# Two cross-attention layers: scores computed a second time in transposed form, heads in groups of four

## The chip, the cores and the metric

The kernel runs on one core of a Trainium2 chip. The core has TensorE (matrix products, into the PSUM banks), VectorE, ScalarE, GpSimd, and SyncE, whose queue issues most of the DMAs. The metric is the device time of one execution in microseconds, the median of the runs.

## The reference

Sixteen sequences ("batches") of 112 tokens of width 320 pass two cross-attention layers over a context of 375 tokens of width 192. Everything is float32.

```python
# layer 0: 8 heads of 40; the context's last 4 tokens are `ca`, the other 371 `enc`
query, keyt, valt = x @ Wq, enc @ Wk, enc @ Wv
hs = mha(query, keyt, valt)                      # softmax over 371 keys
ca_q1 = einsum('btc,th->bch', ca, Wq_ca)[:, indices, :]
ca_hs1 = mha(ca_q1, x, x)                        # softmax over 112 keys
ca_hs2 = mha(ca_hs1 @ Wq, ca @ Wk_ca, ca @ Wv_ca)  # softmax over 4 keys
x1 = (hs + ca_hs2) @ Wout + b_out + x
# layer 1: 20 heads of 16, softmax over all 375 tokens
q, k, v = x1 @ Wq1, ctx @ Wk1, ctx @ Wv1
y = mha(q, k, v) @ Wo1 + bo1 + x1                # the probabilities are scaled by one
```

## The kernel before

Work is laid out in iterations t, one per batch, and each mixes the stages of neighbouring batches: group "c" is layer 0 of batch t, "l" the heads of layer 1 of batch t-1, "n" the preparation of batch t+1, "e" the end of batch t-2. An iteration has 28 steps, one per head: steps 0 to 7 are layer 0's heads, 8 to 27 layer 1's. Iterations -1 to 2 and 15 to 17 are written out, the twelve between stand in a loop of six rounds of two.

A head passes `scores` (a TensorE product, queries on the 112 partitions, keys along the columns of `bankS`), the maximum (VectorE), the exponential with its sum (ScalarE, with the negated maximum as bias), the reciprocal and the normalisation (VectorE, or GpSimd for six heads), `transposes` four steps later (three TensorE transposes of 112x125 into `bankT`, copied to `probT` by ScalarE or VectorE), and `attend` six steps later (probabilities times values, into `bankO0` or `bankO1`). TensorE does two heads at a time.

Projections and small products are the "units". `UNITS` gives each a step, and all share two banks `bankX` in turn, so a unit waits until ScalarE or VectorE has drained the unit two before it. To keep precision, operands are split in a rounded and a rest part (`WH` and `WL`, `ctx_hi` and `ctx_lo`) and the products are float32r matmuls of these parts. The keys are brought into a stacked form, three copies (rest, rounded, rounded) on top of each other, so that one matmul forms a head's scores: 24 small copies per batch for layer 1 (line 375, `k1_stack`) and 9 for layer 0 (line 387, `k0_stack`), issued by SyncE. Units `q0T` and `q1T` transpose the likewise stacked queries.

SyncE's queue is in order: a DMA that waits for a semaphore, or that takes long to issue, holds all behind it. Per batch it has the loads of x, ca, context and padded x, the K1 copies after unit K1_2, the K0 copies after unit K0_2, and four rows of values (`v3_rows`). Output rows leave by GpSimd's queue. The four token keys of the second softmax are appended to the 371 of each layer 0 head (line 820), so `attend` sums both.

Of the kernel before, what the change touches and what calls it, by code (L numbers as in the profile page):

```python
# [5 lines left out]
F32 = mybir.dt.float32  # L19
# [12 lines left out]
P = 128  # L32
# [11 lines left out]
C_ALL = C_WO0 + 4 * HID  # L44
# [15 lines left out]
TSLOTS = 4  # L60

POOL_HEADS = {"prob2": (13, 14, 15, 16), "x1b": (), "xb": (24, 26)}
NORMALISED_BY_POOL = frozenset(sum(POOL_HEADS.values(), ()))

COPIED_BY_DVE = frozenset({7, 8, 9, 11, 15, 21, 23, 24})
FIRST = 3
GQ_STEPS = (9, 11, 12, 13)
TOKEN_STEP = 8
SPLIT_STEPS = (2, 14, 16, 17)
PER_TWO_UNITS, PER_TWO_HEADS = 2 * len(UNITS), 2 * HEADS  # L70


def v1_place(h):

    return 2 * (h // 4) + h % 2, h % 4 // 2


V1_ORDER = sorted(range(H1), key=v1_place)


def groups_of(t):
    return (("n" if t < B - 1 else "") + ("c" if 0 <= t < B else "") + ("l" if 1 <= t <= B else "")
            + ("e" if t >= 2 else ""))


def steps_of(t):

    return ([*range(H0)] if "c" in groups_of(t) else []) + ([*range(H0, HEADS)] if "l" in groups_of(t) else [])


class Iteration:

    def __init__(self, t0, j=0):
        self.t0, self.j, self.t = t0, j, t0 + 2 * j
        self.groups = groups_of(t0)
        self.present = [(s, u) for s, u, g in (UNITS if t0 >= 0 else FIRST_UNITS) if g in self.groups]  # L100
        before = sum(g in groups_of(t) for t in range(-1, t0) for _, _, g in UNITS)
        self.at = {u: before + i for i, (_, u) in enumerate(self.present)}
        self.head_at = {s: sum(len(steps_of(t)) for t in range(t0)) + i for i, s in enumerate(steps_of(t0))}
        self.before = Iteration(t0 - 1, j) if t0 >= 0 else None

    def of(self, step):

        return (self, step) if step >= 0 or self.before is None else (self.before, step + HEADS)

    def units(self, step):  # L110

        it, step = self.of(step)
        return [(it, u) for s, u in it.present if s == step]

    def head(self, step):

        it, step = self.of(step)
        return (it, step) if step in it.head_at else None

    def heads(self, step, more=0):  # L120

        return self.head_at[step] + 1 + more + PER_TWO_HEADS * self.j

    def bank_heads(self, step, more=0):

        return self.head_at[step] // 2 + 1 + more + HEADS * self.j

    def slot_heads(self, step):

        return self.head_at[step] // PSLOTS + 1 + PER_TWO_HEADS // PSLOTS * self.j  # L130

    def batches(self, per, off, extra=0):

        return per * (self.t0 + off) + extra + 2 * per * self.j

    def bank(self, unit):
        return self.at[unit] % 2

    def filled(self, unit):
        return self.at[unit] + 1 + PER_TWO_UNITS * self.j  # L140

    def drained(self, unit):

        return self.at[unit] // 2 + 1 + len(UNITS) * self.j

    def parity(self, off):
        return (self.t0 + off) % 2

    def pairs(self, per, off):

        return per * ((self.t0 + off) // 2 + 1) + per * self.j
# [986 lines left out]
```

## Time and profile before

| | us |
|---|---|
| median of 3 runs | 1012.34 (1012.02 to 1013.36) |
| the profiled execution | 1009.08 |
| its span, first to last instruction | 1007.4 |
| TensorE matmuls busy in it | 899.3 (89%) |
| VectorE, ScalarE, GpSimd busy | 640.9, 628.6, 272.3 |
| mean granted clock of TensorE | 0.909 of full speed |

A busy TensorE is not one at its peak: matmuls are pipelined, so that the distance between the starts of two is shorter than the duration of one. In the timeline, rows that follow each other with the same line and tiles are merged into one with a count, and the distance of two rows' starts is what a block costs. A float32 product is carried out as two instructions, a float32r product and a transpose as one. Names of tiles stand without buffer numbers (`k_stack` is k0_stack or k1_stack).

### The profile page before, as it was taken

To read this page: it belongs to the slowest core of one execution; us is meant where nothing else is said; L and a number is where in the kernel's file an instruction comes from. 1 tells how busy PE (TensorE), PEld (TensorE's weight loads), DVE (VectorE), ACT (ScalarE), POOL (GpSimd) and SP (SyncE) were. 2 spreads that over 40 slices of the span, in tenths; PEclk is the share of its full clock that TensorE was granted. 3 is DMA by queue.
4 is the path that set the end of the run, shared out by engine and by line. 5 is a ranking of instruction groups with operands and counts; after the bars stand their busy time and mean duration, and the time that the engine had idled before them with its cause. 6 is when DMAs were issued, how large, how long until landed. Compare 5 with 4: busy or idle time off the path is not lost.

```text
span 1007.4 us, 23258 instructions
## 1 busy us (share of the span) xinstructions
PE 899.3 (89%) x7048; PEld 721.7 (72%) x7048; DVE 640.9 (64%) x1901; ACT 628.6 (62%) x1958; POOL 272.3 (27%) x312
## 2 busy tenths in 40 slices
PE   5678899998989999888989889889998889899987
PEld 4567677777777778677777777677777777777665
DVE  3353758575765857657586667657676576856753
ACT  2354666666766666666677567666666666766643
POOL 4232223232232223223222232322232223220210
PEclk9588999897989989898999989899899989989966
DMA  5443333131333313123232213333131232312000
GB/s 190 133 83 93 59 92 64 54 76 28 99 58 93 65 58 78 34 82 65 91 65 70 59 30 98 59 93 63 52 81 39 81 65 91 65 59 51 15 7 6
DMA packets 49664, 69.06 MB, mean 69 GB/s; under 512 B 10656, under 2 KB 44064, under 8 KB 49552
## 3 DMA queue, kind: packets, MB, share of 16 engines
q1 hardware_dynamic: 48784, 65.30, 27.4%
q0 software_dynamic: 768, 2.29, 0.7%
q8 instruction: 67, 1.10, 0.5%
q14 instruction: 45, 0.37, 0.1%
HBM read 18.93 MB, written 2.42 MB: 21 GB/s over the span
## 4 chain that ended last, share of the span: by engine, by line
PE 73%; ACT 9%; DVE 8%; issue 6%; SPq 2%; DMA 2%; ACTq 0%; POOL 0%; DVEq 0%
PE bankX L868 23%; PE bankT L1003 16%; PE bankO L1028 15%; PE bankS L994 7%; ACT arena L530 4%; ACT arena L647 3%; DVE arena L822 3%; DVE negmax L764 3%; PE bankS L987 2%; PE bankX L929 2%; SPq L387 2%; PE bankX L977 1%; PE bankX L970 1%; PE bankX L950 1%; DMA k_stack<-stage 1%
## 5 line engine op out<-in xcount | busy, mean ns | idle before, releaser
L764 DVE TENSOR_REDUCE negmax<-bankS 112x1 f32<-112x375 f32 (+1 forms) x448 | 241.6, 540 | 228.6 <-PE bankS L994 177.6
L647 ACT ACTIVATE arena<-bankS,negmax 112x375 f32<-112x375 f32 (+1 forms) x448 | 255.8, 571 | 54.9 <-DVE negmax L764 47.6
L639 ACT ACTIVATE arena<-bankT 125x336 f32<-125x336 f32 x320 | 143.5, 449 | 165.7 <-PE bankT L1003 165.7
L1003 PE MATMUL bankT<-cst,arena 112*125 112x112 f32 x1344 | 215.6, 300 | 0.1
L1003 PEld LDWEIGHTS bankT<-cst,arena 112*125 112x125 f32 x1344 | 182.2, 204 | 33.7 <-issue 33.2
L1028 PE MATMUL bankO<-arena,v 125*32 125x112 f32 (+1 forms) x2688 | 188.5, 279 | 0.0
L822 DVE TENSOR_SCALAR arena<-arena,rsum 112x375 f32<-112x375 f32 (+1 forms) x352 | 176.1, 500 | 2.5
L1028 PEld LDWEIGHTS bankO<-arena,v 125*32 125x32 f32 (+1 forms) x2688 | 132.8, 125 | 45.0 <-issue 36.0
L437 POOL TENSOR_TENSOR arena<-arena,rsum 112x375 f32<-112x375 f32 x96 | 77.2, 809 | 160.8 <-DVE rsum L769 160.6
L994 PE MATMUL bankS<-k_stack,q1T 48*112 48x376 f32 x320 | 93.4, 452 | 4.1 <-ACT arena L647 3.7
L647 ACT ACTIVATION_READ_ACCUMULATOR arena<-bankS,negmax 112x1 f32 x448 | 91.1, 203 | 0.0
L769 DVE RECIPROCAL rsum<-psum_ 112x1 f32<-112x1 f32 x448 | 68.8, 154 | 24.1 <-ACT arena L647 23.5
L868 PE MATMUL bankX<-ctx_hi,WH 128*120 128x376 f32 (+2 forms) x192 | 81.7, 426 | 0.1
L868 PE MATMUL bankX<-ctx_hi,WL 128*120 128x376 f32 (+2 forms) x192 | 76.0, 396 | 0.0
L868 PE MATMUL bankX<-WH,ctx_hi 128*125 128x320 f32 x192 | 67.1, 352 | 9.5 <-ACT v L570 6.5
L479 POOL TENSOR_TENSOR arena<-arena,rsum 112x896 f32<-112x896 f32 x16 | 26.8, 1674 | 177.2 <-DVE rsum L799 177.2
L987 PE MATMUL bankS<-k_stack,q0T 120*112 120x372 f32 x128 | 46.8, 406 | 27.9 <-ACT arena L647 13.1
L994 PEld LDWEIGHTS bankS<-k_stack,q1T 48*112 48x112 f32 x320 | 39.5, 180 | 43.7 <-issue 19.6
L775 DVE COPY arena<-bankT 125x336 f32<-125x336 f32 x128 | 63.2, 494 | 3.7 <-PE bankT L1003 3.7
L413 POOL TENSOR_TENSOR w2bd<-w2s,cst 96x896 fp32r<-96x896 f32 x16 | 26.9, 1680 | 127.8 <-DVE w2s L689 127.7
L868 PE MATMUL bankX<-WL,ctx_hi 128*125 128x320 f32 x192 | 58.8, 314 | 0.0
L929 PE MATMUL bankX<-cst,qn 112*120 112x112 f32 x128 | 21.6, 298 | 40.8 <-ACT arena L530 40.8
(113 smaller groups left out, 1445.3 us busy)
## 6 DMA issues: line engine op xcount, KB each, us to landing
k_stack<-stage SPq DMA_DIRECT2D x96, 176.2 KB
k_stack<-stage SPq DMA_DIRECT2D x192, 70.5 KB, 2.5
k_stack<-stage SPq DMA_DIRECT2D x192, 47.0 KB, 2.1
ctx_raw<-in_ctxT SPq DMA_DIRECT2D x16, 376.0 KB, 3.7
k_stack<-stage SPq DMA_DIRECT2D x48, 117.5 KB
xp<-in_xpad SPq DMA_DIRECT2D x16, 224.0 KB, 3.6
x_raw<-in_xT SPq DMA_DIRECT2D x16, 168.0 KB, 2.5
out<-x1b POOLq DMA_DIRECT2D x16, 140.0 KB, 2.3
```

Source lines behind the costliest of these rows:

```text
L437: nc.gpsimd.tensor_tensor(slot, slot, rsum[:, s:s + 1].broadcast_to((SQ, SK)), ALU.mult)\
L639: nc.scalar.activation(probT[0:KC, h % TSLOTS], bankT[h % 2][0:KC, 0:NKC * SQ] .rearrange("p (k q) -> p k q", k=NKC), ACT.Copy)\
L647: nc.scalar.activation(prob[0:SQ, s % PSLOTS, 0:keys], bankS[s % 2][0:SQ, 0:keys], ACT.Exp, bias=negmax[:, s:s + 1], accum_out=psum_[:, s: ...
L764: nc.vector.tensor_reduce(negmax[:, s:s + 1], bankS[s % 2][0:SQ, 0:keys], axis=AX, op=ALU.max, negate=True).then_inc(max_done, 1)
L769: nc.vector.reciprocal(rsum[:, h:h + 1], psum_[:, h:h + 1]).then_inc(rsum_done, 1)
L775: nc.vector.tensor_copy(probT[0:KC, h % TSLOTS], bankT[h % 2][0:KC, 0:NKC * SQ] .rearrange("p (k q) -> p k q", k=NKC)).then_inc(probT_copi ...
L822: nc.vector.tensor_scalar(slot[:, 0:keys], slot[:, 0:keys], rsum[:, h:h + 1], None, ALU.mult).then_inc(prob_ready[h % PSLOTS], 1)
L868: last = nc.tensor.matmul(dst, lhs, rhs, start=(n == 0), stop=(n == len(passes) - 1))
L987: nc.tensor.matmul(bankS[s % 2][0:SQ, 0:SKE + 1], q0T[:, s, :], k0_stack[:, s, 0:SKE + 1], start=True, stop=True).then_inc(scores_done, 1)
L994: nc.tensor.matmul(bankS[s % 2][0:SQ, 0:SKP], q1T[par][row, h // 2, :], k1_stack[par][row, h // 2, :], start=True, stop=True)\
L1003: last = nc.tensor.transpose(bankT[s % 2][0:KC, k * SQ:(k + 1) * SQ], prob[0:SQ, s % PSLOTS, KC * k:KC * k + KC], ident[0:SQ, 0:SQ])
L1028: mm = nc.tensor.matmul(dst, v, probT[0:KC, h % TSLOTS, k, :], start=(first and k == 0), stop=(last_one and k == NKC - 1))
```

## The change

- *Scores twice.* The scores are computed as before, but only for their maximum. The negated maxima of four heads (112x4) are transposed by TensorE (`transpose_m`), copied to `mT` by VectorE, and SyncE places them by DMA (`place_m`) as one more row under the stacked queries; the stacked keys have a row of ones there. `shifted_scores` then multiplies with keys as the stationary side: its result has keys on the partitions, 125 at a time, and queries along the columns, already less the maximum. One exponential per group of four heads (two in layer 0) goes straight to `PT`, the form that `attend` needs. The transposes of the probabilities, the copies to `probT` and the bias of the exponential are gone.
- *Sums from a ones column.* The value tiles hold a column of ones beside each head, so `attend` also gives the sum. Its result is copied by VectorE to `o0T` or `o1T`, transposed back by TensorE (units N0, N1a, N1b), divided by the sum by VectorE, and transposed once more (hn0T, hn1T) for the output projections.
- *Groups and slots.* An iteration has 7 slots of four heads: slots 0 and 1 are layer 0 of batch t, slots 2 to 6 layer 1 of batch t-1. A group is scored in its slot, its maxima are transposed in the next, its transposed scores and `attend` come in the one after (`LAG` 2). `bankS` holds two heads, `bankST` the transposed scores of one group.
- *Token values.* The four token values are multiplied with the output weights ahead (`out_values`, prologue, rows stored to DRAM and loaded as `gst` per batch); the third softmax enters out0 as a ninth matmul (p3T). out0 has three row blocks instead of four.
- *Unrolled.* The loop is gone; iterations 0 to 17 are written out. SyncE also stores the output.

```diff
+SLOTS, LAG, GROUP = 7, 2, 4
+SLOT_L1 = 2
+M_ROW0, M_ROW1 = 3 * D0, 3 * D1
+UNITS = [
+    ([("W2", 1), ("K1_0", 0)], [("K1_1", 0), ("q1T_0", -1)]),
+    ([("q1T_1", -1), ("q1T_2", -1), ("q0", 1)], [("N1a", -2), ("p3T", 0), ("K1_2", 0)]),
+    ([("V1_0", 0), ("N1b", -2), ("V1_1", 0)], [("hn1T", -2), ("V1_2", 0)]),
+    ([("q0T_0", 1), ("S2_0", 1), ("S2_1", 1)], [("out1", -2)]),
+    ([("K0_0", 1), ("K0_1", 1)], [("N0", 0), ("q0T_1", 1), ("T2_0", 1)]),
+    ([("hn0T", 0), ("T2_1", 1), ("K0_2", 1)], [("out0", 0), ("PV2", 1)]),
+    ([("V0_0", 1), ("x1T", 0)], [("q1", 0), ("S3", 1), ("V0_1", 1), ("V0_2", 1)]),
+]
...
+            def place_m(g):                                    # SyncE
+                layer, b, k = g
+                n = NUMBER[g]
+                src = mT[:, n % MT_BUFS, :].bitcast(F32)
+                sp.wait_ge(mT_copied, n + 1)
+                if layer == 0:
+                    sp.dma_start(q0T[M_ROW0:M_ROW0 + 1, GROUP * k:GROUP * k + GROUP, :].bitcast(F32),
+                                 src.unsqueeze(1)).then_inc(m0_placed, 16)
+                else:
+                    for odd in range(2):
+                        row = 64 * odd + M_ROW1
+                        sp.dma_start(q1T[b % 2][row:row + 1, 2 * k:2 * k + 2, :].bitcast(F32),
+                                     src[2 * odd:2 * odd + 2].unsqueeze(1)).then_inc(m1_placed, 16)
...
+            for t in ITERATIONS:
+                for i in range(SLOTS):
+                    if scored_at(t, i, 1):
+                        place_m(scored_at(t, i, 1))
...
+                    if i == 2 and t < B:
+                        stack_k1(t)
...
+                    if i == 6 and t + 1 < B:
+                        stack_k0(t + 1)
...
-                        nc.scalar.activation(prob[0:SQ, s % PSLOTS, 0:keys], bankS[s % 2][0:SQ, 0:keys], ACT.Exp,
-                                             bias=negmax[:, s:s + 1], accum_out=psum_[:, s:s + 1])\
-                            .then_inc(exp_done, 1)
+                    nc.scalar.activation(dst[0:KC], bankST[0:KC, :, 0:GROUP * SQ], ACT.Exp).then_inc(exp_done, 1)
...
-                        nc.vector.tensor_scalar(slot[:, 0:keys], slot[:, 0:keys], rsum[:, h:h + 1], None,
-                                                ALU.mult).then_inc(prob_ready[h % PSLOTS], 1)
+                nc.vector.tensor_reduce(negmax[:, n % 2, first:first + step + 1:step], bankS[0:SQ, :, 0:keys], axis=AX,
+                                        op=ALU.max, negate=True).then_inc(max_done, 1)
...
-                    last = nc.tensor.transpose(bankT[s % 2][0:KC, k * SQ:(k + 1) * SQ],
-                                               prob[0:SQ, s % PSLOTS, KC * k:KC * k + KC], ident[0:SQ, 0:SQ])
+                if layer == 0:
+                    pe.wait_ge(m0_placed, 16 * (G0 * b + k + 1))
+                else:
+                    pe.wait_ge(m1_placed, 32 * (G1 * b + k + 1))
...
+                                last = nc.tensor.matmul(bankST[0:KC, n_bank, col:col + SQ],
+                                                        k1_stack[b % 2][row, h // 2, KC * c:KC * c + KC],
+                                                        q1T[b % 2][row, h // 2, :], start=True, stop=True)
...
+                    g, before, late = scored_at(t, i), scored_at(t, i, 1), scored_at(t, i, LAG)    # TensorE
+                    if g:
+                        scores(g, 0)
+                    if late:
+                        shifted_scores(late)
+                    if before:
+                        transpose_m(before, NUMBER[late] if late else attended)
...
+                    for u in units_of(t, i, 0):
+                        unit(*u)
+                    if g:
+                        scores(g, 1)
+                    if late:
+                        attend(late, transposed)
...
+                    for u in units_of(t, i, 1):
+                        unit(*u)
```

Three places of the order follow; the square brackets name the semaphores that a row waits for. First SyncE's queue, which issues in this order. One batch before (an unrolled one):

```order
L342 DMA x_raw<-in_xT 128x336 [waits xb_ready]
L344 DMA ca_raw<-in_caS 96x112
L347 DMA ctx_raw<-in_ctxT 128x752
L354 DMA xp<-in_xpad 112x512
L375 DMA k_stack<-stage 16x3x376 [waits bank_drained0]
L375 DMA k_stack<-stage 16x3x376 x11
L375 DMA k_stack<-stage 16x2x376 x12
L387 DMA k_stack<-stage 40x3x376 [waits bank_drained0]
L387 DMA k_stack<-stage 40x3x376 x5
L387 DMA k_stack<-stage 40x2x376 x3
L392 DMA v<-v_rows 4x512
```

The same queue after, from slot 2 of an iteration to slot 5; L346 are the K1 copies, L360 the placings of a layer 1 group's maxima (two per group), L355 that of a layer 0 group's, L403 the output, L306 the load of x:

```order
L355 DMA q0T<-mT 1x4x112 [waits mT_copied]
L346 DMA k_stack<-stage 16x3x376 [waits bank_drained0,st_done]
L346 DMA k_stack<-stage 16x3x376 x11
L346 DMA k_stack<-stage 16x2x376 x12
L360 DMA q1T<-mT 1x2x112 [waits mT_copied]
L360 DMA q1T<-mT 1x2x112
L360 DMA q1T<-mT 1x2x112 [waits mT_copied]
L360 DMA q1T<-mT 1x2x112
L403 DMA out<-x1b 112x320 [waits bank_drained1]
L360 DMA q1T<-mT 1x2x112 [waits mT_copied]
L360 DMA q1T<-mT 1x2x112
```

And from slot 6 to the next iteration's slot 1; L332 are the K0 copies:

```order
L360 DMA q1T<-mT 1x2x112 [waits mT_copied]
L360 DMA q1T<-mT 1x2x112
L332 DMA k_stack<-stage 40x3x376 [waits bank_drained1,st_done]
L332 DMA k_stack<-stage 40x3x376 x5
L332 DMA k_stack<-stage 40x2x376 x3
L360 DMA q1T<-mT 1x2x112 [waits mT_copied]
L360 DMA q1T<-mT 1x2x112
L313 DMA ctx_raw<-in_ctxT 128x752 [waits ctx_split]
```

What moved: between the K1 copies and the K0 copies, where the queue before held nothing of the heads, stand the placings of five groups, each waiting for `mT_copied`; the first of them comes behind all 24 K1 copies.

TensorE, two heads of layer 1 before: value products of an earlier pair, scores of a new pair, transposes of a pair between:

```order
L1028 MATMUL bankO<-arena,v_0 32x112 [waits probT_copied1,probT_copied0]
L1028 MATMUL bankO<-arena,v_0 32x112 x5
L994 MATMUL bankS<-k_stack,q1T 112x376 [waits exp_done] x2
L1003 MATMUL bankT<-cst,arena 125x112 [waits probT_copied0,prob_ready2]
L1003 MATMUL bankT<-cst,arena 125x112 x2
L1003 MATMUL bankT<-cst,arena 125x112 [waits probT_copied1,prob_ready3]
L1003 MATMUL bankT<-cst,arena 125x112 x2
```

TensorE after, slot 4: two heads' scores, the transposed scores of the group of slot 2, the transpose of slot 3's maxima, the units of the slot's first half (the first row of K0_0 is shown; the nine rows to the end of K0_1 are left out here), the other two scores, and the value products:

```order
L1095 MATMUL bankS<-k_stack,q1T 112x376 [waits bank_drained0,max_done]
L1095 MATMUL bankS<-k_stack,q1T 112x376
L1137 MATMUL bankST<-q1T,k_stack 125x112 [waits exp_done,m1_placed]
L1137 MATMUL bankST<-q1T,k_stack 125x112 x8
L1137 MATMUL bankST<-q1T,k_stack 125x112 [waits even_done]
L1137 MATMUL bankST<-q1T,k_stack 125x112 x2
L1108 MATMUL bankO<-cst,negmax 4x112 [waits o_copied,mT_copied,max_done]
L942 MATMUL bankX<-ctx_hi,WH 120x376 [waits ctx_split,bank_drained1]
...
L1095 MATMUL bankS<-k_stack,q1T 112x376 [waits max_done]
L1095 MATMUL bankS<-k_stack,q1T 112x376
L1171 MATMUL bankO<-arena,v_0 32x112 [waits bank_drained1,o_copied,mT_copied,exp_done]
L1171 MATMUL bankO<-arena,v_0 32x112 x11
```

What moved: the transposes of probabilities are gone, and the transposed scores in their place wait for the placed maxima (`m1_placed`) and for the exponential before (`exp_done`).

## Rows read from the trace of the kernel before

**Rows 1.** The page, part 1: engine busy us (share) xinstructions
```profile
PE 899.3 (89%) x7048; PEld 721.7 (72%) x7048; DVE 640.9 (64%) x1901; ACT 628.6 (62%) x1958; POOL 272.3 (27%) x312
```

**Rows 2.** Timeline, GpSimd, w2: start, length, operation, tiles, shape, count [idle before]
```profile
160.86 1.68 POOL L413 TENSOR_TENSOR w2bd<-w2s,cst 96x896 fp32r<-96x896 f32 x1 [7.46 <-DVE w2s L689]
...
865.22 1.68 POOL L413 TENSOR_TENSOR w2bd<-w2s,cst 96x896 fp32r<-96x896 f32 x1 [7.53 <-DVE w2s L689]
```

**Rows 3.** Timeline, SyncE's queue: an unrolled batch, then one of the loop
```profile
158.03 16.47 SPq L375 DMA_DIRECT2D k_stack<-stage  x24
...
496.16 0.33 SPq L344 DMA_DIRECT2D ca_raw<-in_caS  x1
...
510.05 15.87 SPq L375 DMA_DIRECT2D k_stack<-stage  x24
542.18 8.18 SPq L387 DMA_DIRECT2D k_stack<-stage  x9
```

**Rows 4.** Timeline, TensorE, two heads of layer 1 with out0 between
```profile
536.13 0.43 PE L994 MATMUL bankS<-k_stack,q1T 48*112 48x376 f32 x2
536.49 0.91 PE L1003 MATMUL bankT<-cst,arena 112*125 112x112 f32 x6
537.16 0.38 PE L868 MATMUL bankX<-WH,act_hi 128*112 128x320 f32 x1
...
538.99 0.33 PE L868 MATMUL bankX<-ctx_hi,WH 128*80 128x376 f32 x1
...
539.93 0.77 PE L1028 MATMUL bankO<-arena,v 125*32 125x112 f32 x12
540.63 0.43 PE L994 MATMUL bankS<-k_stack,q1T 48*112 48x376 f32 x2
```

**Rows 5.** Timeline, TensorE, layer 0 scores and a K1 block
```profile
503.25 0.59 PE L987 MATMUL bankS<-k_stack,q0T 120*112 120x372 f32 x2
503.68 0.80 PE L1003 MATMUL bankT<-cst,arena 112*125 112x112 f32 x6
504.26 0.42 PE L868 MATMUL bankX<-ctx_hi,WH 128*128 128x376 f32 x1
...
505.19 0.34 PE L868 MATMUL bankX<-ctx_hi,WH 128*128 128x376 f32 x1
```

**Rows 6.** Lines by form: shapes xcount | busy us, mean ns | idle
```profile
L764 DVE TENSOR_REDUCE negmax<-bankS 112x1 f32<-112x375 f32 x320 | 172.9, 541 | 178.9 <-PE bankS L994 177.6
...
L722 DVE TENSOR_REDUCE negmax<-bankX 112x4 f32<-112x448 f32 x32 | 19.5, 611 | 0.0
...
L582 ACT ACTIVATE q0T<-bankX 120x448 fp32r<-120x448 f32 x32 | 17.3, 541 | 8.0 <-PE bankX L929 6.2
```

**Rows 7.** Waits: engine, tile <- releaser: us in total, times, longest
```profile
PE bankS L987 <- issue: 13.1, 5, 2.6
```

**Rows 8.** Issues and landings: K1 copies, then the copy of ca_raw
```profile
L375 SPq DMA_DIRECT2D k_stack<-stage x384: 585/594/1974, 59.5 to 934.3; - x192
...
DMA to landing us min/median/max: 2.1/2.5/3.5
...
DMA to landing us min/median/max: 1.9/2.0/6.2
```

**Rows 9.** TensorE after a wait; last a window: engines busy, granted clock, DMA
```profile
529.71 0.50 PE L929 MATMUL bankX<-cst,qn 112*120 112x112 f32 x3 [1.97 <-ACT arena L530]
...
533.20 0.52 PE L868 MATMUL bankX<-ctx_lo,WH 128*120 128x376 f32 x1
533.51 0.52 PE L868 MATMUL bankX<-ctx_hi,WL 128*120 128x376 f32 x1
...
532.00:536.00 4.00, 4.00 (x28) 3.71 (x26) 2.37 (x8) 2.33 (x8) 3.09 (x3) 0.69 0.02 4
```

**Rows 10.** Timeline, prologue: SyncE's K0 copies, TensorE's first scores
```profile
37.26 8.57 SPq L387 DMA_DIRECT2D k_stack<-stage  x9
...
52.75 0.96 PE L987 MATMUL bankS<-k_stack,q0T 120*112 120x372 f32 x2 [1.10 <-DMA k_stack<-stage]
```

More of the change, by code:

```diff
@@ L86, in steps_of @@
[L86 to L151, printed above, removed]
@@ new lines, with units_of @@
+C_ALL = C_WO0 + 3 * HID
+SLOTS, LAG, GROUP = 7, 2, 4
+G0, G1 = H0 // GROUP, H1 // GROUP
+SLOT_L1 = 2
+M_ROW0, M_ROW1 = 3 * D0, 3 * D1
+DMAS_K0, DMAS_K1 = 9, 24
+MT_BUFS = 4
+UNITS = [
[7 rows of a table added]
+]
+FIRST_UNITS = ["W2", "q0", "K0_0", "K0_1", "K0_2", "S2_0", "S2_1", "q0T_0", "q0T_1", "T2_0", "T2_1", "PV2", "S3",
+               "V0_0", "V0_1", "V0_2"]
+ITERATIONS = range(0, B + 2)
+def units_of(t, i, phase):
+    return [(name, t + off) for name, off in UNITS[i][phase]
+            if 0 <= t + off < B and not (off == 1 and t < 0)]
@@ new lines, in filled, with bank, drained, scored_at @@
+def filled(name, b):
+    return AT[name, b] + 1
+def bank(name, b):
+    return AT[name, b] % 2
+def drained(name, b):
+    return AT[name, b] // 2 + 1
+def scored_at(t, i, before=0):
+    n = SLOTS * t + i - before
+    return SCORED.get((n // SLOTS, n % SLOTS))
+def heads_of(g):
+    layer, _, k = g
+    return range(GROUP * k, GROUP * k + GROUP)
+def m_column(layer, j):
+    return j if layer == 0 else 2 * (j % 2) + j // 2
+def st_place(layer, j, c):
+    if layer == 0:
+        return c, SQ * j
+    odd, pair = j % 2, j // 2
+    return (odd, SQ * (2 * c + pair)) if c < 2 else (2, SQ * (2 * odd + pair))
@@ L305, in xattn_kernel @@
         p3_ready = sem("p3_ready")
[L306 to L317 removed]
+        p3_rounded = sem("p3_rounded")
+        p3_split = sem("p3_split")
+        rec_done = sem("rec_done")
+        hn0_ready = sem("hn0_ready")
+        hn1_ready = sem("hn1_ready")
+        out_stored = [sem(f"out_stored{i}") for i in range(2)]
+        pool_chain = sem("pool_chain")
+        splits = {u: n for n, u in enumerate(u for u in ORDER if u[0] in ("hn0T", "x1T", "hn1T"))}
+        recips = {u: n for n, u in enumerate(u for u in ORDER if u[0] in ("N0", "N1a", "N1b"))}
         block = ctx.enter_context(nc.Block())
@@ L398, in _ @@
+            for i in range(2):
+                sp.wait_ge(out_stored[i], 16 * (B // 2))
         @block.gpsimd
         def _(pool):
[L400 to L401 removed]
             def rounded(hi, src):
@@ new lines, in _ @@
+            round_weights(0)
+            unit("W2", 0)
+            round_weights(1)
+            unit("q0", 0)
+            for i in range(3):
+                unit(f"K0_{i}", 0)
+            exps2(0, 0)
+            exps2(0, 1)
+            unit("q0T_0", 0)
+            unit("q0T_1", 0)
+            round_weights(2)
+            unit("T2_0", 0)
+            unit("T2_1", 0)
+            round_weights(3)
+            unit("PV2", 0)
+            round_weights(4)
+            unit("S3", 0)
+            for m in range(4):
+                round_g(m)
@@ new lines, in _ @@
+            for name in FIRST_UNITS[:7]:
+                unit(name, 0)
+            token_products()
+            unit("q0T_0", 0)
+            unit("q0T_1", 0)
+            for m in range(4):
+                query_keys(m)
+            unit("T2_0", 0)
+            unit("T2_1", 0)
+            unit("PV2", 0)
+            unit("S3", 0)
+            for m in range(4):
+                out_values(m)
+            for i in range(3):
+                unit(f"V0_{i}", 0)
+            attended = transposed = 0
```

1194 lines of the change are left out of this document (654 added, 540 removed).

## The prediction

> **What bounds the kernel now.** I read the page's engine totals, the start times of an instruction that occurs once per batch, then SyncE's and TensorE's timelines over one batch, the waits, and the landings. TensorE's matmuls are busy 899.3 of 1007.4 us, no other engine more than 641 [rows 1]. The expansion of w2 runs once per batch on GpSimd: from 160.86 to 865.22 us there are 12 batches, 58.7 us each [rows 2]. That period is TensorE's own work. SyncE has room: it issues the 24 K1 copies of a batch in 15.87 us, the 9 K0 copies in 8.18 and four small loads, and idles for the rest [rows 3]; nothing urgent stands behind them in its queue.
>
> **What TensorE does, before and after.** Two heads cost before: scores 0.36 (536.13 to 536.49), six transposes 0.67, value products 0.70 (539.93 to 540.63) [rows 4]; in layer 0 the scores take 0.43 [rows 5]. Four heads cost about 3.5 us. Afterwards, in my names:
> - SC, scores of two heads, twice per group: as now, 0.43 taken for both layers.
> - SH, the transposed scores: 12 matmuls with 125 stationary and 112 moving columns. The nearest row are the transposes, also 125 and 112, 0.11 us apart [rows 4]. Layer 0 (121 rows of the array): 12 x 0.11 + 0.1 = 1.4. In layer 1 two heads lie in separate halves of the rows, as the scores pair does: from 0.7, if they overlap, to 1.4; I take 1.0. The float32r rate at 112 columns stands in no row; at the rate of the float32 value products (six in 0.70, two abreast, so 0.2 each) SH would be 1.2 and 2.4, my upper ends.
> - TM, the transpose of the four maxima: 0.2, one transpose and the start of a block.
> - AT, the value products: layer 1 puts four column groups abreast where two were, so 0.7 for four heads if that works, 1.4 (as now) if not; I take 0.7. Layer 0 keeps two, 1.3.
>
> A layer 1 group costs 2.8 for 3.5, a layer 0 group 3.8 for 3.9. Per batch that saves 5 x 0.7 + 2 x 0.1 = 3.7. The added transposes (N0, N1a, N1b, hn0T, hn1T, p3T: 19 at 0.1 and six block starts) cost 2.4, three matmuls fewer in out0 give back 0.45 (twelve take 1.83, 537.16 to 538.99 [rows 4]). Net gain 1.7 us per batch, 27 us in all. ScalarE and VectorE are relieved far more: 28 exponentials become seven of 1.3 to 1.5 (448 columns take 541 ns, 1344 at that slope 1.3 us), and the normalisations and copies of probT go. The maximum over two heads, 750 columns, takes 0.95, from 541 ns at 375 and 611 at 448 [rows 6]. They did not bound the kernel, so this buys only slack, and so do GpSimd's six multiplications fewer. Unrolling removes the 2.6 us that TensorE loses at each of five returns of the loop, 13.1 us [rows 7].
>
> **What is put on SyncE.** This decides. A group's negated maxima must reach one row of q0T or q1T by DMA (`place_m`) before its SH, two slots after its scores. Those DMAs stand in SyncE's one queue, in order, with the stacking. A small copy takes 0.33 to issue [rows 3] and 2.0 to land; a K1 copy 0.59, landing 2.5 after its start [rows 8]. Two places:
>
> *K1 chain.* In slot 2 SyncE waits for the maxima of slot 1 (SC 0.4, SH 1.4, TM 0.2, copy 0.3: 2.3 after the slot's start), places them (0.4), then issues the 24 K1 copies, 16.1 (15.87 here, 16.47 in an unrolled batch [rows 3]). Only then, 18.8 us after slot 2 began, can it place the maxima of slot 2's group: a second issue and a landing make 21.2. TensorE wants them one SC into slot 4. Slots 2 and 3 hold SC 1.7, SH 2.8, TM 0.4, AT 2.6, V1 and small blocks 3.0, q0T, S2 and out1 2.9, and 1.6 where blocks wait for a bank that ScalarE drains only after the exponentials: 15. So TensorE stands about 6 us. SH is at the head of its queue, so all of TensorE waits, and the other engines for it.
>
> *K0 chain.* In slot 6 the placing of slot 5's maxima (2.0 + 0.8) precedes the nine K0 copies: 8.2 to issue, the last landing about 2.1 after the issue ends (no row shows a K0 landing; K1's are 2.1 to 3.5 after their start). 13.1 us pass from slot 6's start until the next batch's scores may begin. Slot 6 holds 8.6 us of TensorE (a group 2.8, V0 2.4, x1T, q1 and S3 2.6, waits 0.8). It stands 4.5 more.
>
> **The period.** A, slots 0 and 1: 2 x (two SC, SH 1.0, TM, AT) = 5.5; W2 0.8; three K1 blocks at 0.93 (504.26 to 505.19 [rows 5]); q0 1.3; q1T, N1a, p3T 2.0; two waits for banks, 1.1 where q0 needs q1T_1's copy, which stands behind the exponentials, and 0.6 where K1_2 needs N1a's: 14.1. B, from SH in slot 4 to slot 6: two groups less one SC 5.1, three K0 blocks 2.8, out0 1.4, PV2 0.9, N0, q0T_1, T2 twice and hn0T 2.4, waits of 0.9 and 1.5 of the same kind: 15.0. At full clock 14.1 + 21.2 + 15.0 + 13.1 = 63.4.
>
> The clock: before, TensorE works at the lower level (1.2 GHz) after a wait of 1.97 us: matmuls of the K0 block start 0.31 apart, where a K1 block of five takes 0.93 at the upper level, and the granted clock of 532 to 536 is 0.69 [rows 9]. Each batch now has two such stands, both longer. I take 3.5 us of wall time at the low level after each, which loses half of it: 2 x 1.75 = 3.5. The period is 66.9, against 58.7.
>
> Two rules of the Trainium skill bear on SH. The transposes use nearly all rows of the array for both load and product and still start 0.11 us apart [rows 4]. By "TensorE: Matmul & The Clock Gate", Part 3 (the mechanism), a weight load overlaps a running matmul only where the row group differs. By that rule layer 0's SH would be 12 x (0.10 + 0.05) = 1.8, an estimate from that page, and the total 6 us higher through the K1 chain; the trace disagrees. The pair of layer 1 scores, in two row halves, takes 0.36 where layer 0's pair takes 0.43 [rows 4, 5], so the trace shows some overlap. By "TensorEngine Tiling (Array Packing)", Key Properties, different tiles load and multiply in parallel; by that rule layer 1's SH is 0.7 and the total 17 us lower (four SH of A and B, 14 batches).
>
> **Ends of the run.** Before, the first scores stand at 52.75, released by the K0 copies issued from 37.26 [rows 10]. The new prologue adds the out_values products, 24 instructions of 320 columns at 0.27 (320/112 of 0.09), some at the low clock: 9. Then batch 1's x loads only behind 12 stores, and K1 and K0 copies go out back to back (16 + 8, and a landing): iteration 1 starts near 104. Iterations 1 to 14 at 66.9, less 3 since iteration 1 has no late groups in slots 0 and 1: 934. Iteration 15, with the K1 chain and no K0: 50. Iterations 16 and 17, in which each slot waits for its maxima's round trip of 4 to 5 us: 43. Span 104 + 934 + 50 + 43 = 1131. The profiled execution has 1009.08 for its span of 1007.4, so 1133; the median of the runs is 3.3 above the profiled one: **1136**.
>
> **Rivals.**
> 1. *The placings find room (faster).* If the maxima are not late, the period is TensorE's own: 14.1 + 15 + 15.0 + 8.6 + 1.5 for the clock = 54; iteration 1 then starts near 96: 96 + 14 x 54 - 3 + 80 = 929, with 5 for the rest 934. For it: 1.7 us less work and the slack of two engines. Against it: 24 issues take 15.9 to 16.5 us in every batch, and the placing behind them is two slots from its use. 0.14.
> 2. *The chains hold, the rest is tighter.* Without the bank waits (4.1) and the loss of clock (3.5) the period is 59.3, the total 1136 - 14 x 7.6 = 1030, and 10 less with the ends as tight. It decides at a period of 58.5; 0.09, of it 0.02 within 0.2% and 0.01 below.
> 3. *The new forms on TensorE run slow.* SH at 1.2 and 2.4, the chains grow by 1.0 and 0.2, A and B by 0.8: the period is 68.9 and with the clock 69.5: 1172; AT at 1.4 in layer 1 gives 2.8 a period, the same. No float32r matmul under 320 columns and no four groups abreast are in the trace. 0.12.
> 4. The forecast: 0.65, own range 1090 to 1165.
>
> The range for 8 in 10 is 1035 to 1188: its lower end leaves out rival 1 and part of 2. A measurement of this kernel can tell 0.2%, 2 us, from no change. Faster 0.15, same 0.02, slower 0.83.
>
> **What would show it.** Right: TensorE idle 5 to 8 us once per batch ahead of slot 4's transposed scores, released by the DMA of the maxima, and 3 to 6 us ahead of the next batch's first scores, released by the K0 copies; SyncE issuing 16 us in one stretch before the first; the granted clock down after both; ScalarE and VectorE under half busy. If these two waits are absent, the step on SyncE is wrong, and with it the sign. If SH in layer 1 takes 0.7 or 1.4, only its size is off. If the period is right and the time is not, the ends are.

## The result and the profile after

| | median us | runs | profiled span |
|---|---|---|---|
| before | 1012.18 | 4, 1004.97 to 1013.36 | 1007.4 |
| after | 1200.97 | 4, 1197.09 to 1202.04 | 1195.3 |

The changed kernel takes 1.1876 of the time before (95% interval 1.1814 to 1.1938). It is slower, as forecast, but by 189 us where 124 were forecast, and 13 us above the upper end of the range. Ratios with an interval, here and below, leave out runs more than 1.5% above the fastest of their kernel; of e2, e6 and e8 too few are left for one.

The page of the kernel after, parts 1, 2 (two of its lines) and 4, beside [rows 1]:

```profile
PE 890.2 (74%) x7400; PEld 712.3 (60%) x7400; DVE 457.4 (38%) x979; ACT 400.1 (33%) x922; POOL 193.3 (16%) x206
PE   6767678778787877777787767777777786777686
PEclk9778788878878787778868888978787897888875
PE 46%; SPq 22%; issue 11%; DVE 9%; ACT 8%; DMA 4%; ACTq 0%; DVEq 0%
PE bankX L942 21%; SPq L346 19%; PE bankST L1137 7%; PE bankO L1171 4%; PE bankS L1091 2%; ACT arena L548 2%; DVE negmax L736 2%; DMA q1T<-mT 2%; PE bankS L1095 2%; PE bankX L1041 2%; DVE qn L727 1%; PE bankX L1061 1%; DVE hn L760 1%; DVE act_lo L820 1%; SPq L360 1%
```

VectorE and ScalarE lost 184 and 229 us of work, as meant. TensorE is now busy for 74% of the span where it was busy for 89%. The chain that ended last spends 22% of the span in SyncE's queue, 19% in the one line L346, which issues the K1 copies. No engine bounds this kernel. An order does.

TensorE's longest groups of waits, after (total, times, longest):

```profile
PE bankS L1091 <- issue: 79.8, 15, 5.5
PE bankST L1137 <- DMA q1T<-mT: 72.2, 15, 7.6
```

Once per batch each, at the two places that the prediction names. The first is the next batch's first scores, held by the K0 copies (the profile names no releaser and says "issue"). The second is slot 4's transposed scores, held by the DMA of the maxima. Rows of SyncE's queue around the batch that begins at 598.43, to be read beside [rows 3] (start, length, line, operation, count; the rows between are left out):

```profile
586.11 1.17 SPq L360 DMA_DIRECT2D q1T<-mT  x2
587.38 8.61 SPq L332 DMA_DIRECT2D k_stack<-stage  x9
619.73 0.58 SPq L355 DMA_DIRECT2D q0T<-mT  x1
620.41 16.67 SPq L346 DMA_DIRECT2D k_stack<-stage  x24
637.13 1.33 SPq L360 DMA_DIRECT2D q1T<-mT  x2
```

And TensorE at the ends of these two chains (in brackets the idle time before, and what ended it):

```profile
592.61 0.31 PE L942 MATMUL bankX<-WL,ctx_hi 128*125 128x320 f32 x1
598.43 0.93 PE L1091 MATMUL bankS<-k_stack,q0T 120*112 120x372 f32 x2 [5.51 <-issue]
599.30 1.51 PE L1137 MATMUL bankST<-q1T,k_stack 49*125 49x112 f32 x12
600.88 1.57 PE L1041 MATMUL bankX<-x_raw,bd 128*96 128x112 f32 x6
639.49 1.51 PE L1137 MATMUL bankST<-q1T,k_stack 49*125 49x112 f32 x12 [4.11 <-DMA q1T<-mT]
```

The placing of slot 2's maxima leaves SyncE at 637.13, right behind 24 copies that began at 620.41, and TensorE goes on at 639.49. The nine K0 copies end at 596.0, and the next batch's scores start at 598.43. What these copies read was ready at 580.68, when VectorE had drained K0's last part; the maxima of the placing ahead of them came 5.4 us later, at 586.08:

```profile
580.14 0.55 DVE L777 TENSOR_TENSOR stage<-bankX,stage 80x376 fp32r<-80x376 f32 x1 [1.69 <-ACT stage L585]
585.83 0.25 DVE L742 CAST mT<-bankO 4x112 fp32r<-4x112 f32 x1
```

The twelve transposed products behind either stand take 1.51 us. In slot 5 of the batch before, at the upper clock, the same twelve take half as long:

```profile
575.22 0.81 PE L1137 MATMUL bankST<-q1T,k_stack 49*125 49x112 f32 x12
```

TensorE's stretches behind the stands (a stand is one of these two waits), one row each (window, length, busy time of PE, PEld, DVE, ACT, POOL, granted clock, DMA share, GB/s):

```profile
596.70:606.90 10.20, 8.47 (x54) 6.71 (x55) 3.13 (x6) 2.04 (x3) 1.68 (x1) 0.50 0.24 73
606.90:617.20 10.30, 8.02 (x79) 6.36 (x78) 3.79 (x9) 4.34 (x8) 0.00 (x0) 1.00 0.05 14
617.20:627.40 10.20, 9.89 (x56) 8.47 (x56) 3.33 (x8) 2.73 (x6) 0.00 (x0) 0.50 0.40 61
637.60:644.50 6.90, 5.01 (x25) 4.47 (x25) 0.81 (x2) 1.82 (x3) 0.00 (x0) 0.51 0.11 28
```

The clock is at its lower level (0.50 of 2.4 GHz, so 1.2) behind both stands, and in a third stretch, 617.20 to 627.40, ahead of which TensorE had only short waits for banks (1.05 us before 611.00, 1.23 before 615.39). Over iterations 1 to 14 it is 0.82, the first row here; the second is the run `e5_both` below, which has neither stand:

```profile
109.10:1096.20 987.10, 744.03 (x6309) 600.84 (x6309) 381.30 (x830) 338.94 (x794) 151.85 (x163) 0.82 0.24 57
```
```profile
115.70:869.60 753.90, 643.74 (x6309) 523.16 (x6310) 376.44 (x829) 334.76 (x792) 151.73 (x163) 0.94 0.32 75
```

The same 6309 matmuls over 14 periods are busy 53.1 us a period after, 46.0 without the stands. So 7.1 us a period of busy time goes with the lower clock, beside 9.5 of standing itself (152.0 us of waits in the two groups above against 9.4 in `e5_both`, divided by 15).

I divided the batch as the prediction did, from the start times of the scores and of the transposed scores, and took means over 13 batches. K1 chain is slot 2's start to slot 4's transposed scores, K0 chain slot 6's start to the next batch's scores, A and B what lies between. All in us:

| | A | K1 chain | B | K0 chain | period |
|---|---|---|---|---|---|
| forecast, full clock | 14.1 | 21.2 | 15.0 | 13.1 | 63.4 (+3.5 for the clock) |
| after | 18.1 | 21.8 | 17.4 | 13.8 | 71.1 |
| e1, K0 copies first | 14.3 | 21.7 | 17.4 | 8.5 | 62.0 |
| e2, K1 copies spread | 17.9 | 17.2 | 15.6 | 13.8 | 64.5 |
| e5, both | 14.7 | 16.1 | 14.8 | 8.6 | 54.2 |
| e4, chains kept, TensorE kept busy | 14.7 | 21.6 | 16.6 | 13.9 | 66.6 |
| e3, placings on ScalarE's queue | 14.6 | 17.9 | 16.7 | 9.0 | 58.2 |
| e6, e5 with x earlier | 14.3 | 16.1 | 15.2 | 8.4 | 54.0 |
| e8, e6 with hn0T last | 14.6 | 16.1 | 13.2 | 8.7 | 52.6 |
| e9, e8 with q0 in the middle | 12.9 | 16.0 | 13.2 | 8.5 | 50.6 |

### The profile page after: what moved, and what is told of

Same layout as the page of the kernel before. It is cut to its first block, busy times and chain, and to the rows that moved or that the text cites. A ratio compares the mean times of both kernels' runs of the same rounds, so it can differ in the third digit from the quotient of the medians.

```text
span 1195.3 us, 19120 instructions
## 1 busy us (share of the span) xinstructions
PE 890.2 (74%) x7400; PEld 712.3 (60%) x7400; DVE 457.4 (38%) x979; ACT 400.1 (33%) x922; POOL 193.3 (16%) x206
## 4 chain that ended last, share of the span: by engine, by line
PE 46%; SPq 22%; issue 11%; DVE 9%; ACT 8%; DMA 4%; ACTq 0%; DVEq 0%
PE bankX L942 21%; SPq L346 19%; PE bankST L1137 7%; PE bankO L1171 4%; PE bankS L1091 2%; ACT arena L548 2%; DVE negmax L736 2%; DMA q1T<-mT 2%; PE bankS L1095 2%; PE bankX L1041 2%; DVE qn L727 1%; PE bankX L1061 1%; DVE hn L760 1%; DVE act_lo L820 1%; SPq L360 1%
## 5 line engine op out<-in xcount | busy, mean ns | idle before, releaser
L736 DVE TENSOR_REDUCE negmax<-bankS 112x2 f32<-112x750 f32 (+1 forms) x224 | 208.5, 931 | 141.5 <-PE bankS L1091 82.2
L548 ACT ACTIVATE arena<-bankST 125x1344 f32<-125x1344 f32 x80 | 103.3, 1292 | 282.8 <-PE bankST L1137 282.7
L1171 PE MATMUL bankO<-arena,v 125*32 125x112 f32 (+2 forms) x2688 | 138.6, 317 | 8.3 <-ACT arena L548 7.3
L1137 PE MATMUL bankST<-q1T,k_stack 49*125 49x112 f32 x960 | 89.2, 330 | 72.4 <-DMA q1T<-mT 72.2
L1137 PEld LDWEIGHTS bankST<-q1T,k_stack 49*125 49x125 f32 x960 | 83.4, 243 | 88.0 <-DMA q1T<-mT 78.0
L1171 PEld LDWEIGHTS bankO<-arena,v 125*32 125x32 f32 (+2 forms) x2688 | 106.1, 144 | 39.0 <-issue 24.3
L942 PEld LDWEIGHTS bankX<-ctx_hi,WH 128*120 128x120 f32 (+2 forms) x192 | 47.4, 247 | 56.7 <-DVE act_hi L823 26.4
L1091 PEld LDWEIGHTS bankS<-k_stack,q0T 120*112 120x112 f32 x128 | 27.0, 239 | 83.8 <-issue 83.3
L474 POOL TENSOR_TENSOR x1b<-x,bias_sb 112x320 f32<-112x320 f32 x16 | 13.9, 867 | 366.5 <-DVE x L817 366.5
L742 DVE CAST mT<-bankO 4x112 fp32r<-4x112 f32 x112 | 28.9, 258 | 108.6 <-PE bankO L1108 108.5
L942 PE MATMUL bankX<-WH,act_hi 128*112 128x320 f32 x144 | 56.1, 390 | 11.4 <-DVE act_hi L823 10.0
## 6 DMA issues: line engine op xcount, KB each, us to landing
k_stack<-stage SPq DMA_DIRECT2D x192, 70.5 KB, 2.5
```

What stands on the lines that cost most here:

```text
L548: nc.scalar.activation(dst[0:KC], bankST[0:KC, :, 0:GROUP * SQ], ACT.Exp).then_inc(exp_done, 1)
L736: nc.vector.tensor_reduce(negmax[:, n % 2, first:first + step + 1:step], bankS[0:SQ, :, 0:keys], axis=AX, op=ALU.max, negate=True).then_in ...
L742: nc.vector.tensor_copy(mT[:, n % MT_BUFS, :], bank_mT).then_inc(mT_copied, 1)
L942: last = nc.tensor.matmul(dst, lhs, rhs, start=(n == 0), stop=(n == len(passes) - 1))
L1091: last = nc.tensor.matmul(bankS[0:SQ, j, 0:SKE + 1], q0T[0:M_ROW0, h, :], k0_stack[0:M_ROW0, h, 0:SKE + 1], start=True, stop=True)
L1137: last = nc.tensor.matmul(bankST[0:KC, n_bank, col:col + SQ], k1_stack[b % 2][row, h // 2, KC * c:KC * c + KC], q1T[b % 2][row, h // 2, :] ...
```

## The experiments

Medians are compared with the kernel before on the same chip: 1013.3 for e1, e2, e4 and e5, 1013.1 for e3, e6, e7 and e8, 1010.3 for e9 and e10.

**e1: K0's copies ahead of slot 6's placings.**

```
                 for i in range(SLOTS):
+                    if i == 6 and t + 1 < B:
+                        stack_k0(t + 1)
                     if scored_at(t, i, 1):
                         place_m(scored_at(t, i, 1))
...
-                    if i == 6 and t + 1 < B:
-                        stack_k0(t + 1)
```

> Edit: in slot 6 SyncE issues the nine K0 copies ahead of the two placings of that slot, nothing else. The chain theory (C: two chains through SyncE's queue set the period) expects the copies to start when K0's last part is evicted (about 4 us before slot 6) and to be down before the next batch's scores ask for them: the 5.5 us wait of TensorE ahead of L1091 goes, the chain from slot 6 to those scores falls from 13.9 to about 8.4 us, and 15 batches give 82 us, so about 1118 us, less a few us a batch if TensorE's clock stays up behind the missing wait (1070 to 1120). The load theory (L: TensorE's own added work sets the period and the waits only take up its slack) expects the wait to come back elsewhere and a time within 20 us of 1201.

Measured: 1080.2 (1069.1 to 1082.4), 121 us less than after and inside the forecast of theory C. In the table the K0 chain falls from 13.8 to 8.5, and A, in which nothing was edited, from 18.1 to 14.3. B, behind the other stand, stays at 17.4. The wait at L1137 grew, since TensorE now comes to it sooner:

```profile
PE bankST L1137 <- DMA q1T<-mT: 87.3, 15, 7.2
```

The load theory (L) is out. Per batch 5.3 us went from the K0 chain, the stand, and 3.8 from A, where the mean granted clock rose from 0.76 to 0.99 and the waits stayed at 2.2 us.

**e2: K1's copies in three parts.**

```
-                    if i == 2 and t < B:
-                        stack_k1(t)
+                    if i in (2, 3, 4) and t < B:
+                        stack_k1(t, {2: (0, 1, 2), 3: (3, 4, 5), 4: (6, 7)}[i])
```
(`stack_k1` takes the heads' rows of its part, and waits only ahead of the first)

> Edit: the 24 K1 copies go out in three parts of nine, nine and six, behind the placings of slots 2, 3 and 4, instead of all behind the one of slot 2. Theory C expects the placing of slot 3 to leave SyncE some 10 us sooner, so that the wait of 3.6 to 4.1 us in slot 4 at L1137 goes, the stretch slot 2 to slot 4 falls from 23.0 to about 19 us, and 16 batches give about 64 us: 1137 us, or 1090 to 1137 with a share of the clock. Theory L expects about 1201.

Measured: 1099.8 (1081.8 to 1103.6), 101 less than after and within the forecast; 72 was the whole of the wait removed. The K1 chain falls by 4.6 and B by 1.8, while A stays at 17.9, behind the stand that is left:

```profile
PE bankS L1092 <- issue: 80.6, 15, 6.0
PE bankST L1138 <- DMA q1T<-mT: 1.0, 1, 1.0
```

**e5: both.** The edits of e1 and e2 together.

> Edit: both of the foregoing. Theory C with a clock term (waits leave TensorE at its lower level for some 10 us behind each) expects 5.5 + 4.1 us a batch for the waits and 4 to 6 us a batch for the clock: a period of 71.5 - 9.6 - 5 = 57 us and 1201 - 16 x 14.6 = about 967 us; without a clock term 1201 - 16 x 9.6 = 1047 us. The difference between the two (80 us) is what this run is to tell apart. Theory L expects no less than 1180.

Measured: 957.9 (953.1 to 964.8), 0.9436 of before (0.9397 to 0.9476). This is within 10 us of the theory with a clock term, and 90 from the one without. The two edits gave 121 and 101 alone and 243 together. The changed kernel is thus faster than the old one once these two orders are mended (some 7 us of that are the unrolling, by e7). The period, 54.2, is what the prediction's first rival had worked out for TensorE's own work with a little loss of clock (54).

**e4: both chains kept, TensorE kept busy in them.** The added products are not part of the computation, and what they write is overwritten.

```
+            def fill(dst, count):
+                pe.wait_ge(w_split, 5)
+                for _ in range(count):
+                    nc.tensor.matmul(dst, WH[:, 0:P], WH[:, 0:HID], start=True, stop=True)
...
                     if k == 0:
+                        if b > 0:
+                            fill(bankS[:, 0, 0:HID], 30)
                         pe.wait_ge(k0_stacked, 16 * DMAS_K0 * (b + 1))
...
+                    if k == 0:
+                        pe.wait_ge(exp_done, n)
+                        fill(bankST[:, 0, 0:HID], 20)
                     pe.wait_ge(m1_placed, 32 * (G1 * b + k + 1))
```

> Edit: both chains stay, but TensorE is given products of the weight table with itself (320 columns each, their result is overwritten by the next use of the bank) to run in the two waits: 30 ahead of the wait for K0's copies, 20 ahead of the wait for the placing in slot 4. At the higher clock they take about 4 and 2.7 us, no more than the waits. If my prediction failed because its clock term was too small, the stretches behind the waits now run at the higher clock and the period loses 4 to 7 us: 1090 to 1140 us. If the stretches A and B are long for another reason (waits for banks that DVE and ACT drain), the time stays within 15 us of 1201, or grows by the dummy products' overrun.

Measured: 1143.8 (1138.9 to 1156.8), 57 us less than after, with some 700 matmuls more. The forecast of 1090 to 1140 missed by 4 us; the direction is clear. This run separates the terms best: the chains keep their lengths (21.6 and 13.9), and A falls to 14.7, as in e5, where the stand is gone. The rows behind the K0 chain, to be read beside those of after:

```profile
570.05 4.56 PE L1076 MATMUL bankS<-WH 128*128 128x320 f32 x30
575.62 0.59 PE L1098 MATMUL bankS<-k_stack,q0T 120*112 120x372 f32 x2 [1.01 <-DMA k_stack<-stage]
576.13 0.90 PE L1147 MATMUL bankST<-q1T,k_stack 49*125 49x112 f32 x12
577.06 0.91 PE L1041 MATMUL bankX<-x_raw,bd 128*96 128x112 f32 x6
```

Scores, transposed scores and W2 take 0.59, 0.90 and 0.91 where after they take 0.93, 1.51 and 1.57. A wait of 1.01 us right behind 4.56 us of work did not bring the clock down there. B fell only to 16.6. Its filler left 2.8 us of wait a batch ahead of it (41.9 in all), and the clock stayed low in it: 0.83 on the mean, for 0.78 after and 0.95 in e5, while TensorE's waits inside B are 2.1 to 2.4 us in all three.

**e3: the placings issued from ScalarE's queue.**

```
                         exps(scored_at(t, i, LAG))
+                    if scored_at(t, i, 1):
+                        place_m(scored_at(t, i, 1))
```
(in ScalarE's program, with its DMAs on that queue; the two lines on SyncE's go)

> Edit: the placings go out from ScalarE's queue, each behind the exponentials of its slot; the copies stay on SyncE where they are. If the wait in slot 4 comes from the order on SyncE's queue (the placing of slot 3 is issued behind 24 copies), it goes as it did with the copies spread, though all 24 still go out in one piece: 4.1 us x 16 less, and K0's copies start some 1 us sooner, so 1201 - 66 - 16 = 1119 us without the clock and 1080 to 1120 with a share of it. If it comes from the copies' traffic (the placing's 448 bytes land late because 24 transfers are under way), the wait of 3.6 to 4.1 us in slot 4 stays and the time stays near 1185 us.

Measured: 1007.3 (1001.1 to 1021.7), 0.9935 of before (0.99 to 0.997). The traffic theory is out: 24 copies still leave in one piece, and the wait in slot 4 is gone. Both theories' numbers missed by over 70 us, since I had K0's copies start only 1 us sooner. They start when K0's last part is drained, 5.4 us before slot 6's placing had its maxima in the rows of after; a queue that never waits for maxima doesn't hold them. SyncE's and ScalarE's queues in this run:

```profile
538.43 16.28 SPq L346 DMA_DIRECT2D k_stack<-stage  x24
567.50 8.22 SPq L332 DMA_DIRECT2D k_stack<-stage  x9
```
```profile
504.06 1.17 ACTq L531 DMA_DIRECT2D q1T<-mT  x2
```

It is 49 us slower than e5. 1.17 us of issue for each group of layer 1 now stands ahead of ScalarE's copies out of PSUM, and TensorE's largest wait for a bank grows, first this run's row, then e5's:

```profile
PE bankX L942 <- DVE act_hi L823: 50.3, 31, 2.2
```
```profile
PE bankX L943 <- DVE act_hi L824: 32.8, 30, 1.6
```

That is 17.5 of the 49 us. The granted clock of batches 1 to 14 is also lower, 0.90 for 0.94; how much of that the placings cause isn't shown, and the profiled execution is the longest of the ten.

**e6: e5, and batch 1's x loaded ahead of `stack_k0(0)`.**

> Edit: both reorderings of the copies, and in the prologue the load of x of batch 1 goes out ahead of stack_k0(0) and of the twelve stores of the token products instead of behind them. TensorE waits 13.8 us for that load ahead of L1042 in the run with both reorderings. If nothing else is late there, 10 to 13 us go: 958 - 12 = 946 us. If the slots behind are held by the stores and K0's copies themselves, the wait comes back within the next slots and the time is 955 to 958 us.

Measured: 963.0 (944.5 to 971.6), against 957.9 for e5: with runs 27 us apart, no gain can be told. The wait for x went from 18.0 to 4.3 us in all, and another took its place, for GpSimd's split of x (`PE bankX L943 <- POOL x_hi L439: 17.2, 1, 17.2`). GpSimd was late because its clearing of `v1`, ahead of the split in its program, waits for the stores of the token products:

```profile
73.56 1.70 POOL L506 MEMSET v<- 128x1920 f32 x1 [16.82 <-DMA g_rows<-v]
```

So the second outcome is the one that the trace bears out.

**e7: the kernel before, unrolled.** `whole_run` becomes a plain loop over `range(-1, B + 2)`.

> Edit, to the kernel before: its sixteen iterations are written out instead of run in a hardware loop over pairs, nothing else. My prediction put the loop at 13.1 us (five returns of 2.6 us); it expects 1012 - 13 = 999 us. If the returns lie beside other waits it stays within 3 us of 1012; if straight code brings fetch stalls of its own, it is slower.

Measured: 1009.7 (997.4 to 1013.5), 0.9929 (0.9884 to 0.9973). Unrolling is worth 7 us with 3 to 12 as its interval, where I had 13.1. The wait of [rows 7] is gone from the trace. But the matmuls of the twelve batches that had stood in the loop are busy longer at a lower granted clock, first before, then this run:

```profile
104.68:808.28 703.60, 646.25 (x5236) 520.70 (x5236) 469.38 (x1414) 463.96 (x1463) 198.03 (x228) 0.93 0.29 67
```
```profile
108.53:803.69 695.16, 651.03 (x5236) 523.67 (x5236) 466.95 (x1414) 465.25 (x1463) 198.24 (x227) 0.91 0.29 68
```

**e8: e6, with hn0T last in slot 5's first phase.**

```
-    ([("hn0T", 0), ("T2_1", 1), ("K0_2", 1)], [("out0", 0), ("PV2", 1)]),
+    ([("T2_1", 1), ("K0_2", 1), ("hn0T", 0)], [("out0", 0), ("PV2", 1)]),
```

> Edit, on top of the kernel with both reorderings and the early load: in slot 5 the transposes hn0T come last in the first phase instead of first, so that the short draining of its bank (ACT L638, DVE L821 and L824) lies beside two heads' scores and an attend and not ahead of K0_2. Theory: what is left of the period (53.3 us) are TensorE's own work and waits for banks, and each of those that is hidden comes off the end; here 1.6 us go, out0 then waits some 0.8 us for the same draining, 12 to 24 us over 15 batches against the kernel without this edit: 922 to 934 us. Rival: the period is held by the three chains of SyncE again, now tighter; then no gain beyond 3 us.

Measured: 942.4. Of its four runs 930.9 and 932.0 lie in the forecast of 922 to 934, 952.8 and 955.9 above it; e6's shortest is 944.5, so the gain over e6 is nearer 13 us than the 21 between the medians. Against e6, B falls from 15.2 to 13.2. TensorE's waits in B fall by only 0.9 of that, since out0 now waits, as expected; the granted clock in B goes from 0.92 to 1.00.

**e9: e8, with q0 between q1T_1 and q1T_2.**

```
-    ([("q1T_1", -1), ("q1T_2", -1), ("q0", 1)], [("N1a", -2), ("p3T", 0), ("K1_2", 0)]),
+    ([("q1T_1", -1), ("q0", 1), ("q1T_2", -1)], [("N1a", -2), ("p3T", 0), ("K1_2", 0)]),
```

> Edit, on top of the kernel with hn0T last: in slot 1 the query product q0 goes between the transposes q1T_1 and q1T_2 instead of behind both. It now waits for the bank of x1T's product two units earlier and no longer for q1T_1's draining by ScalarE, 1.05 us in each of 14 batches; what waits for q1T_2's bank comes behind an attend. Theory of the bank waits: 10 to 15 us less than the kernel without it (930 to 942), so 918 to 930 us. Rival: within 3 us of it.

Measured: 915.4 (913.5 to 919.5), **0.9072 of before** (0.9036 to 0.9107). This is the fastest version, 3 us below its forecast of 918 to 930. A falls from 14.6 (e8) to 12.9, more than the wait of 1.05: the waits inside A fall by 1.4, from 2.2 to 0.7, since the one for `hn` got shorter too. The granted clock in A goes from 0.97 to 0.99. What of the remaining 0.3 us is the clock's, no run separates.

**e10: e9, with q0T_0 behind S2_0 and S2_1.**

> Edit, on top of that: in slot 3 the transposes q0T_0 come behind the two score products S2_0 and S2_1 instead of ahead. S2_1 no longer waits 1.19 us for q0T_0's draining; q0T_0 waits for S2_0's bank instead, whose draining by DVE is not in the rows yet in this order. Theory: 0.5 to 1.2 us in each of 15 batches, 8 to 18 us below e9. Rival: the wait only changes its name, within 3 us of e9.

Measured: 927.9, 0.9197 of before (0.9151 to 0.9243), so 12 us slower than e9: neither theory. (One of its six runs, 1341.6, stands apart and is not explained.) The wait did not only change its name, it grew. Ahead of q0T_0 TensorE now waits 2.3 us for ScalarE to drain S2's bank, where S2_1 waited 1.3; first e10's row, then e9's:

```profile
PE bankX L1007 <- ACT arena L555: 34.2, 15, 2.3
```
```profile
PE bankX L1048 <- ACT q0T L619: 17.9, 15, 1.3
```

## Why the prediction was right in sign and wrong in size

**Right: what is put on SyncE.** Both waits stand where they were forecast, once per batch, 4.8 and 5.3 us on the mean (6 and 4.5 forecast), and each goes with the order that was said to cause it. With both orders mended the kernel is faster than before (e5), so the two chains, with the clock behind them, turn the sign. Their lengths were forecast as 21.2 and 13.1, and are 21.8 and 13.8. A part of this, 0.3 and 0.5, is the placing's issue: one DMA takes about 0.6 and two 1.17 to 1.33, where the sums had 0.4 and 0.8, from `ca_raw` [rows 3]. The price of a K1 copy (0.59 [rows 8]) stood closer, and holds for a DMA of 0.9 KB too. In the K0 chain the scores start 2.6 us after the last issue ends (2.1 forecast), and the maxima come 0.4 us sooner.

**Right: TensorE's new forms.** At the upper clock SH takes 0.74 in layer 1 (I took 1.0) and 1.34 in layer 0 (1.4), AT 0.71 and 1.31 (0.7 and 1.3), from one block's start to the next. The rule by which layer 0's SH would take 1.8 ("TensorE: Matmul & The Clock Gate" of the Trainium skill, Part 3) is not borne out by the new trace either. The rule of "TensorEngine Tiling (Array Packing)" of the Trainium skill, Key Properties, by which layer 1's would take 0.7, is. Rival 3, which had these forms slow, is out. Its sum was also off: its 68.9 has the clock in it already, so by its own terms the time is 1136 + 14 x 2.0 = 1164, and not 1172.

**Wrong: the step "The clock".** I took 3.5 us at the low level after each stand and called its cost 2 x 1.75 = 3.5 a batch. A was forecast at 14.1 and took 18.1, B at 15.0 and took 17.4: 6.4 in place of 3.5. That is 2.9 a batch (about 0.6 of it is A's own work: 14.7 in e5 for 14.1), and with the chains' 1.3 it is the difference of the periods, 71.1 against 66.9. Iterations 1 to 14 took 987.1 us for the 934 forecast: 53 of the 65 us that were missing.

That it is the clock, and not waits for banks, is read from the five runs together. Means over the same 13 batches, with the granted clock of each stretch and TensorE's waits (over 0.15 us) inside it:

| | A us | clock | waits | B us | clock | waits |
|---|---|---|---|---|---|---|
| after | 18.1 | 0.76 | 2.2 | 17.4 | 0.78 | 2.1 |
| e1, no stand ahead of A | 14.3 | 0.99 | 2.2 | 17.4 | 0.77 | 2.2 |
| e2, no stand ahead of B | 17.9 | 0.77 | 2.2 | 15.6 | 0.89 | 2.4 |
| e5, neither | 14.7 | 0.96 | 2.2 | 14.8 | 0.95 | 2.4 |
| e4, stands filled | 14.7 | 0.98 | 2.3 | 16.6 | 0.83 | 2.2 |

The waits inside A and B hardly change; their lengths follow the clock. For A the cause is shown twice: e1 takes its stand away, and e4 leaves the chain's length as it is and gives TensorE something to do in it. For B it is shown by e2 and e5, and only in part by e4.

The duration had been read from one stretch behind a wait of 1.97 us in the kernel before [rows 9], and that was a short one. One iteration earlier and one later TensorE waits 1.97 and 1.98 us at the same place, and there the level is low for 6.7 us each time:

```profile
589.20:595.90 6.70, 6.22 (x31) 5.34 (x32) 2.25 (x7) 3.05 (x12) 1.94 (x2) 0.50 0.01 2
473.10:479.80 6.70, 6.70 (x33) 5.65 (x34) 2.80 (x8) 3.02 (x8) 3.21 (x3) 0.50 0.01 2
```

In the kernel after, behind a stand of 5.5 us, it stayed low for the whole of 596.70 to 606.90, and fell again at 617.20. A granted clock of 0.82 on two levels, 0.5 and 1, over a period of 71.1 is some 26 us a batch at the low level, about 16 of them in A and B, where I took 7. So 3.5 should have been an end of the range and not the value. The range had nothing above the forecast for this term: the one rival that was slower, rival 3, was about the new forms, and that was the wrong unknown.

**The ends of the run.** Iteration 1 started at 109.1 (104 forecast), after a wait of 14.1 us for batch 1's x, which the prediction had seen as an order of loads and priced too low. What follows the first scores of iteration 15 took 99 us (93 forecast). Together that is the remaining 11 us.

**Unrolling.** 13.1 were forecast, about 7 measured (e7), the interval just short of the forecast. The returns' idle time went as forecast, but the matmuls of the loop's batches were busy 4.8 us more (651.03 for 646.25), at 0.91 of full clock for 0.93; what lowered the clock isn't shown. The sum did not rest on it, since the period was built up from its parts.

**Rival 1** gave 934 for the case that the placings find room. Made to find it (e5), the kernel takes 957.9: its period was right (54 and 54.2), and its ends were not (iteration 1 at 115.7 for 96, and 93 us from iteration 15 on for 80).

## What to carry to other kernels

Put a short transfer that TensorE waits for on a queue with nothing long ahead of it, or cut the long series into parts and issue the short one between them. Look also at what a queue's own wait holds back: here nine copies whose data lay ready stood behind a placing whose maxima were not. And price a stand of TensorE at more than its length. Here 9.5 us of standing a batch came with 7.1 more of busy time in the same matmuls, so range that term by itself, from nothing to the whole next stretch at half clock, and look at more than one place of the trace for its length. Where the stand can't be removed, work in it whose result is thrown away can give some of that back (57 us here).

## What the hardware showed that was not expected

- Behind a stand of 5.5 us TensorE was at 1.2 GHz for the whole of 596.70 to 606.90, and was busy for 8.47 us of these 10.2. The level also fell at 617.20, where the waits before had been 1.05 and 1.23 us.
- At the same wait of 2 us, three iterations of the kernel before show low stretches of 3.4, 6.7 and 6.7 us.
- 20 and 30 products whose results are thrown away made the kernel 57 us faster.
- The issue of a DMA on SyncE or ScalarE took about 0.6 us for the 0.9 KB of a placing, as much as for a K1 copy of 47 to 70.5 KB, while `ca_raw` took 0.43 in the same kernel. Among these, size doesn't set it.
